# Weight chunks through two buffers of magnitudes and four raw ones, the loads in another order, and the first two steps reordered on every engine

## What is computed

```
_quant_weight(w):  s = max(|w|, row) / 127;  q = round(w / s)                    # wq, wo
_qlinear(..., W):  Wr = W[:, idx];  w_scale = max(|Wr|, row) / 448;  qw = fp8(Wr / w_scale)   # w_gate, w_up, w_down
q = w8a8(layernorm(x), wq, bq);  k = ctx @ wk.T + bk;  v = ctx @ wv.T + bv        # 16 heads of 32
o = softmax(q k^T / sqrt(32) + mask) v
x = x + tanh(g_xattn) * w8a8(o, wo, bo)
h = layernorm(x);  g, u = fp8linear(h, w_gate), fp8linear(h, w_up)                # 1408 wide
x = x + tanh(g_ffn) * fp8linear(silu(g) * u, w_down)
```

## Time and profile before

| | |
|---|---|
| runs before | 606.95 us median of 3 (601.56 to 607.03) |
| profiled execution | 608.15 us |
| its span | 606.4 us |
| busy share of the span | PE 87%, DVE 85%, ACT 79%, POOL 37% |
| granted TensorE clock, mean | 0.942 |
| step 0 / step 1 / a steady step | about 75.7 / 68.7 / 59.2 us |

### The profile page before, as it was taken

How to read it: one execution, slowest core, us unless ns; L and a number is a source line. 1 busy time by engine, 2 the same in 40 slices (tenths; PEclk the granted TensorE clock), 3 DMA queues, 4 the chain that set the end, 5 groups by cost and what they waited for, 6 DMA issues and landing times.

```text
span 606.4 us, 10842 instructions
## 1 busy us (share of the span) xinstructions
PE 525.3 (87%) x3456; PEld 332.3 (55%) x3456; DVE 513.5 (85%) x1290; ACT 477.2 (79%) x1160; POOL 223.4 (37%) x210
## 2 busy tenths in 40 slices
PE   0667878798999999999999999999999998877834
PEld 0655556556755675567556755765576555443311
DVE  3699985879889988998999899979997996599794
ACT  0697996999888898888988898889798987683341
POOL 1332333002281438234724471546164513361420
PEclk9898996998999999999999999999999998685888
DMA  7822523110001010101010101010100000000000
GB/s 273 273 88 70 157 70 97 69 53 2 36 1 54 36 36 2 52 36 36 2 53 36 35 2 54 36 36 1 53 37 1 1 2 35 1 2 0 35 1 35
DMA packets 15240, 28.75 MB, mean 47 GB/s; under 512 B 3792, under 2 KB 5840, under 8 KB 15184
## 3 DMA queue, kind: packets, MB, share of 16 engines
q1 hardware_dynamic: 8640, 14.68, 7.2%
q0 software_dynamic: 3488, 12.85, 6.5%
q10 hardware_dynamic: 3056, 0.54, 0.5%
HBM read 23.87 MB, written 4.19 MB: 46 GB/s over the span
## 4 chain that ended last, share of the span: by engine, by line
PE 51%; DVE 21%; ACT 13%; issue 10%; ACTq 2%; DMA 1%; POOL 1%; DVEq 0%; POOLq 0%
PE bank_s L794 7%; PE bank_t L853 7%; PE bank_u L814 5%; PE bank_g L814 5%; PE bank_a L801 4%; PE bank_g L801 4%; DVE prob L1265 3%; PE bank_o L895 2%; DVE q L1180 2%; DVE t_sb L1175 2%; DVE t_sb L1219 2%; ACT prob L597 2%; PE bank_a L825 2%; PE bank_g L1029 2%; DVE ts L1450 2%
## 5 line engine op out<-in xcount | busy, mean ns | idle before, releaser
L597 ACT ACTIVATE prob<-prob,neg_max 128x256 f32<-128x256 f32 x256 | 127.2, 503 | 2.8 <-DVE neg_max L1265 2.7
L1265 DVE CUSTOM_DVE_ANT_0 prob<-bank_s,mask_sb 128x256 f32<-128x256 f32 x256 | 96.6, 420 | 22.1 <-PE bank_s L794 8.5
L608 ACT ACTIVATE probT<-bank_t 128x512 f32<-128x512 f32 x128 | 73.5, 588 | 19.9 <-PE bank_t L853 16.7
L385 POOL TENSOR_TENSOR up<-up,wgu_scale 128x512 f32<-128x512 f32 (+1 forms) x42 | 54.7, 1303 | 89.5 <-ACT up L577 89.5
L853 PE MATMUL bank_t<-ident,prob 128*128 128x128 f32 x512 | 79.2, 283 | 8.8 <-ACT prob L597 7.9
L853 PEld LDWEIGHTS bank_t<-ident,prob 128*128 128x128 f32 x512 | 59.3, 143 | 35.9 <-issue 17.2
L794 PE MATMUL bank_s<-kf,qf 32*128 32x256 f32 x512 | 75.3, 413 | 3.0 <-DVE neg_max L1265 2.9
L794 PEld LDWEIGHTS bank_s<-kf,qf 32*128 32x128 f32 x512 | 45.2, 190 | 27.0 <-issue 18.3
L395 POOL TENSOR_TENSOR up<-gate,up 128x512 f32<-128x512 f32 (+1 forms) x42 | 54.4, 1295 | 4.6 <-DVE gate L1325 1.9
L400 POOL TENSOR_TENSOR x<-x,y 128x512 f32<-128x512 f32 x14 | 19.6, 1398 | 97.8 <-DVE y L1463 97.8
L597 ACT ACTIVATION_READ_ACCUMULATOR prob<-prob,neg_max 128x1 f32 x256 | 49.9, 195 | 0.0
(11 more groups left out here) (254 smaller groups left out, 1212.7 us busy)
## 6 DMA issues: line engine op xcount, KB each, us to landing
x_in<-in_x_dram SPq DMA_DIRECT2D x8, 512.0 KB, 3.4
c_in<-in_ctx_dram SPq DMA_DIRECT2D x8, 512.0 KB, 3.5
out_dram<-x POOLq DMA_DIRECT2D x7, 512.0 KB, 3.2
t_sb<-in_L_ffn_w_down_dram POOLq DMA_DIRECT2D x4, 704.0 KB, 6.0
mask_sb<-in_mask_BxSxS_ff_dram SPq DMA_DIRECT2D x8, 256.0 KB, 3.7
kf<-in_L_xattn_wq_dram SPq DMA_DIRECT2D x1, 1024.0 KB, 6.6
probT<-in_L_xattn_wk_dram SPq DMA_DIRECT2D x1, 1024.0 KB, 13.3
qf<-in_L_xattn_wv_dram SPq DMA_DIRECT2D x1, 1024.0 KB, 17.5
```

The costliest lines, as they stand in the source:

```text
L385: pool.tensor_tensor(up[:, c % 2, 0:w], up[:, c % 2, 0:w], wu_scale[:, off:off + w], ALU.mult).then_inc(f["u_scaled"], 1)
L597: ins = act.activation(prob[:, head_par, t, :], prob[:, head_par, t, :], ACT.Exp, bias=neg_max[:, head_par, t:t + 1], scale=-1.0, accum_ou ...
L608: act.activation(probT[:, (slot + 3) % 4, :, :].rearrange("p a b -> p (a b)"), T_BANK[(slot + 1) % 2][:, :], ACT.Copy).then_inc(s["turned_ ...
L1265: ins = dve.tensor_tensor_reduce(prob[:, hp, t, :], S_BANK[hp][:, t * L:(t + 1) * L], mask_sb[:, hb, t, :], -1.0, 3.4e38, ALU.add, ALU.min ...
```

## The change

The edits go together:

- **Units and buffers.** Magnitudes alternate between `mag` with `th` (even k) and `q8_last` seen as 32-bit (odd k). Raw data go through four buffers in turn, k % 4. The rounded unit goes to a new tile `unit_h`, alternating, no longer to `up`. The order of units is down 0, down 1, pair 0, pair 1, down 2, down 3, pairs 2 to 10.
- **Waits.** `mag_unit(k)` waits for unit k-2 to be rounded, the load of unit k for unit k-4, the second pass of `round_unit(k)` for unit k-2 to be turned.
- **Loads.** SP issues down 0 and down 1 ahead of wq, wk after wq, then x and ctx, wv, the gates, bo, bv, wo, bk, bq and the mask. ACT issues the index alone. POOL's first load is pair 0.
- **Order.** The prologue's parts become blocks of step 0, and steps 0 and 1 have another order on every engine. Steady steps and the tail are as before.

```diff
+        unit_h = sb("unit_h", [P, 2, I], BF16)
-        UNITS = [("down", 0), ("down", 1)] + [("pair", c) for c in range(IC)] + [("down", r) for r in range(2, CC)]
+        PAIRS = [("pair", c) for c in range(IC)]
+        UNITS = [("down", 0), ("down", 1)] + PAIRS[0:2] + [("down", 2), ("down", 3)] + PAIRS[2:]
+        raws = (t_sb[:, 0, :], t_sb[:, 1, :], gate[:, :, :].rearrange("p a b -> p (a b)"), x2[:, :, :].rearrange("p a b -> p (a b)"))
         def unit_raw(k):
+            return raws[k % 4][:, 0:2 * C if UNITS[k][0] == "pair" else I]
         def unit_parts(k):
+            w = 2 * C if UNITS[k][0] == "pair" else I
+            if k % 2:
+                return [(0, w, q8_last[:, :].bitcast(F32))]
...
         @block.sync
+            for k in range(2):
+                sp.dma_start(unit_raw(k), w_down[UNITS[k][1] * P:(UNITS[k][1] + 1) * P, :]).then_inc(unit_loaded(k)[0], 16)
             load8("q", wq)
-            load8("k", wk)
...
         @block.gpsimd
-            load_unit(0)
-            pool.wait_ge(s["x_loaded"], 16)
-            load_unit(1)
             pool.wait_ge(s["index_loaded"], 16)
             load_unit(2)
             load_unit(3)
-                        pool.wait_ge(s["wf_ready"], 1 if k == 4 else k - 2)
+                        pool.wait_ge(s["wf_ready"], k - 3)
...
             def mag_unit(k):
-                need(act, s["wf_ready"], k)
+                need(act, s["wf_ready"], k - 1)
             def round_unit(k):
-                need(dve, s["wf_turned"], k - 1 if UNITS[k][0] == UNITS[k - 1][0] == "pair" else k)
+                need(dve, s["wf_turned"], k - 1)
```

More of the change, by code:

```diff
@@ L252, in unit_loaded @@
         def unit_loaded(k):
-            kind, n = UNITS[k]
-            return (s[f"wf_loaded_{n % 3}"], 32 * (n // 3 + 1)) if kind == "pair" else (s[f"wf_loaded_{3 + n % 2}"], 16 * (n // 2 + 1))
+            if k < 2:
+                return s[f"first_loaded_{k}"], 16
+            return s[f"wf_loaded_{k % 4}"], sum(32 if UNITS[j][0] == "pair" else 16 for j in range(k % 4, k + 1, 4) if j >= 2)
         def unit_at(u, first):
@@ L311, in _, with load_unit @@
         def _(pool):
+            def load_unit(k):
+                kind, n = UNITS[k]
+                if kind == "down":
+                    pool.dma_start(unit_raw(k), w_down[n * P:(n + 1) * P, :]).then_inc(unit_loaded(k)[0], 16)
+                else:
+                    for m, src in enumerate((w_gate, w_up)):
+                        pool.indirect_dma_start(unit_raw(k)[:, m * C:(m + 1) * C], None, src,
+                                                bass.IndirectOffsetOnAxis(ap=index[:, n:n + 1], axis=0)).then_inc(unit_loaded(k)[0], 16)
             for name in ("out_ready",):
@@ L324, in _ @@
             pool.wait_ge(s["pow_const"], 1)
-            def load_unit(k):
-                kind, n = UNITS[k]
-                if kind == "down":
-                    pool.dma_start(unit_raw(k), w_down[n * P:(n + 1) * P, :]).then_inc(unit_loaded(k)[0], 16)
-                else:
-                    for m, src in enumerate((w_gate, w_up)):
-                        pool.indirect_dma_start(pair_raw[n % 3][:, m * C:(m + 1) * C], None, src,
-                                                bass.IndirectOffsetOnAxis(ap=index[:, n:n + 1], axis=0)).then_inc(unit_loaded(k)[0], 16)
-            load_unit(0)
-            pool.wait_ge(s["x_loaded"], 16)
-            load_unit(1)
             pool.wait_ge(s["index_loaded"], 16)
@@ L434, in _ @@
         def _(act):
+            act.dma_start(index[:, :], down_index.rearrange("(c p) -> p c", p=P), allow_slow_non_contiguous=True).then_inc(s["index_loaded"], 16)
             for name in ("tT_out_act", "u_ready"):
@@ L462, in mag_unit @@
                 act.wait_ge(s["wf_scaled"], 4 * k + 4)
-                need(act, s["wf_ready"], k)
+                need(act, s["wf_ready"], k - 1)
                 raw = unit_raw(k)
                 if UNITS[k][0] == "pair":
+                    m = unit_parts(k)[0][2]
                     for n in range(2):
-                        act.activation(mag[:, n, :], raw[:, n * C:(n + 1) * C], ACT.Abs, scale=wf_r[:, k % 3, 1, n:n + 1])
+                        act.activation(m[:, n * C:(n + 1) * C], raw[:, n * C:(n + 1) * C], ACT.Abs, scale=wf_r[:, k % 3, 1, n:n + 1])
                     for n in range(2):
@@ new lines, in first_step_order @@
+                k.pro_turn_k(0); k.ctxT_turn(0); k.ctxT_turn(1); k.pro_turn_q(0); k.k_project_even(2)
+                k.k_project_odd(2); k.k_project_even(3); k.k_project_odd(3); k.unit_turn(2); k.xT_turn(4)
+                k.pro_turn_v(1); k.unit_turn(4); k.wo_scale_turn(5); k.xT_turn(5); k.pro_turn_o(4); k.unit_turn(6)
+                k.sx_turn(6); k.q_project_0(6); k.q_project_1(7); k.unit_turn(8); k.first_score(11); k.unit_turn(10)
+                k.v_project_low(10); k.head_score(13); k.head_turn(13); k.head_turn(14); k.unit_turn(12)
@@ L1227, in x2_job, with unit_scale_0, pro_scale_q, pro_k @@
                     return JOBS * B2 + t, mag[:, t, :], rows[:, t, :], xq[:, t, :], C
+                def unit_scale_0(slot):
+                    scale_unit(0)
+                def pro_scale_q(slot):
+                    scale8("q", 0)
+                def pro_k(slot):
+                    pro_evac("k")
+                def pro_int_q(slot):
+                    int8("q", 0)
+                def unit_round_0(slot):
+                    round_unit(0)
+                def pro_q(slot):
+                    pro_evac("q")
                 def pro_v(slot):
                     pro_evac("v")
+                def pro_scale_o(slot):
                     scale8("o", 1)
```

179 lines of the change are left out of this document (88 added, 91 removed).

## The result

The changed kernel takes 602.8 us (median of 20 runs, 597.94 to 606.12), the kernel before beside it 608.32 us (20 runs, 601.27 to 611.27). The ratio is 0.9924, with a 95% interval of 0.9895 to 0.9953; a second series gave 0.9911 (0.9872 to 0.9949). So the change saves 0.8 to 0.9%, some 5 us, where I had forecast 8.4. The profiled execution takes 601.54 us with a span of 599.8.

What follows compares the result with a forecast made beforehand. Steps 0 and 1, with ACT's start and idle time, were taken as what the change can shorten: 7.4 start + 112.5 work + 12.9 + 3.2 idle = 136.0 against 144.4 us, 8.4 earlier, so 599 us; range 591 to 607.

Steps and rivals of the forecast that it cites:

- The new wait: Step 0, ACT at the tanh of the gates: idle from 22 to 31 us for bq, 9 us, bounds 5 and 14.
- ACT idle from there to step 1: Rest of step 0 behind the tanh: 1.8 us of idle time on ACT, bounds 0.5 and 4.
- Start of ACT: Step 0: ACT's first activation at 7.4 us instead of 16.7, 9.3 us earlier, bounds 6.4 and 9.
- only some 4 of it were the constants' fault: Tanh wait: PE's k projection would release the copy only at 27.2 us anyway, so 5 of 9 us aren't the constants'.
- I leave 1.2 us for what comes in its place, beside the other 2.0 us.: ACT in step 1: 3.2 us idle in place of 6.0, bounds 1.5 and 6.5.
- away whole: ACT's 4.0 us wait for step 1's k projection, traced to late unit 10, goes entirely with earlier loading.
- Steady steps and tail follow unchanged: Behind step 2's begin: everything keeps its length, so the 8.4 us gained ahead carries to the total.
- rivals of small gain at 605: Steps 0 and 1: constants' wait takes most of the gain (chance 0.22), or the change does little (0.08); both 605 us.
- late constants: Tanh in step 0, first rival at 605: bq lands at 36 us in place of 31, taking back 5 us.
- a new wait in step 1 worth 3.3 us: Step 1, first rival at 605: a new wait as long as the old one takes back 3.3 us.
- The deeper gain: Rival, steps 0 and 1: small constants before 27.2 us and 1.5 us idle in step 1 give 593 us; chance 0.15.
- no wait of 4 us on L528: Sign in step 1's profile: ACT's 4.0 us wait for the k projection no longer appears.

Runs made afterwards that it cites:

- const_sp: The changed kernel, with SP issuing the gates, bk and bq right behind wk instead of behind wv and wo; 598.31 us, ratio 0.981.
- the pair of repeats: The changed kernel and its version with constants right behind wk, each unedited and once more on one chip; 601.39 us (0.9911) and 602.08 us (0.9891).
- old_act: The changed kernel, with ACT issuing all seven small loads again ahead of its first work, SP none; 604.34 us, ratio 0.9916.
- old_mag: The changed kernel, with magnitudes of unit k waiting for unit k-1 again, as with one buffer; 609.7 us, ratio 1.0008.
- old_step1: The changed kernel, with step 1 in its old order on every engine, except one exchange on PE; 607.72 us, ratio 0.9969.
- old_load: The changed kernel, with the load of unit k waiting for unit k-3, as with three raw buffers; 623.85 us, ratio 1.025.
- before_again: The kernel before the change, unedited, run and profiled once more; 609.31 us, ratio 0.9987.
- its variants: Constants-early version with DVE scaling unit 2 ahead of wo (600.95 us), or POOL's step 1 bias addition moved later (603.05 us) or behind all loads (603.22 us).

## Why the prediction came out too high

What came out too high is the gain. The new wait at the tanh was foreseen rightly, and a size behind it was not. Set against the changed kernel's two executions, from the tanh on:

| us | forecast | first | second |
|---|---|---|---|
| ACT starts | 7.4 | 7.38 | 7.30 |
| tanh, bq landed | 31 | 31.16 | 32.06 |
| ACT idle from there to step 1 | 1.8 | 3.4 | 1.2 |
| ACT idle in step 1 | 3.2 | 5.4 | 5.0 |
| ACT's work from the tanh on | 100.0 | 99.7 | 99.6 |
| step 2 begins | 136.0 | 139.84 | 137.85 |

The idle times are the windows' lengths less ACT's busy time; for the second execution the window from 31.2 to 73.9 has 40.67 of 42.7 us busy, of which 0.86 idle lie ahead of the tanh.

- **Start of ACT**: right to 0.1 us, with the down unit at 5.28 and DVE's 2.1 us, but in part by luck. The DMA moved 304 and 323 GB/s from 2 to 4 and 4 to 6 us, not 250 and 209, so some 1.0 MB had moved when the 0.72 MB of down 0 were there: a higher rate, shared with the loads behind it.
- **The new wait**: its end at 31 was right; it is 10.7 us and not 9 because ACT came at 20.5 and not 22, which costs nothing. The rate of 0.37 MB a us held to 20.4 us (373 GB/s from 7.4 on); over the whole stretch to the tanh, 7.4 to 31.16, it was 344. That only some 4 of it were the constants' fault held as well: const_sp gives 3.2 us back at the rounding of x, and the pair of repeats 4.3 (33.26 and 28.95). By the 358 GB/s of the Trainium skill ("DMA: Bandwidth & Descriptors", Specifications) the prediction's estimate had bq at about 32. The two executions have 31.16 and 32.06, so the landing decides nothing. The window of 373 GB/s stands above the figure, which is no contradiction: the page works it out as half of a stack's 716 GB/s, one of two cores' shares, and this kernel runs on one core. The prediction took it for a limit of a core alone.
- **Where the gain came from**: here the reasoning was weaker than the sum. The sum booked 9.3 us to the start and took 3.7 back in idle time of step 0. old_act shows that a start 7.5 us later gives the same time. On ACT's account of the first execution the 4.6 us are 9.3 of start, less 6.2 of more idle time in step 0, plus 0.9 of less work, which the prediction had put at nothing, and 0.6 of less idle time in step 1. What the gain can't do without is the second magnitude buffer (old_mag, 6 to 8 us), the order of step 1 (old_step1, 5 to 7 at the begin of step 2, some 3 by the ratios) and the fourth raw buffer (old_load, 20). Added up, these prices are several times what the change brings: at least the buffers are worth this only in the new order. The order of step 0 and the early index were not undone by themselves.
- **The step that failed: "I leave 1.2 us for what comes in its place, beside the other 2.0 us."** Idle time of ACT in step 1 is 5.4 and 5.0 us in place of 3.2. The k copy's wait is 2.1 and 0.7, but the turned units (1.6 and 1.8), the masks (1.3 and 0.5) and, in the second execution, the turned probabilities (1.8) stand beside it. So beside the k copy's wait there are 3.3 and 4.3 us, where the prediction had "the other 2.0 us". That ACT, with a shorter step, meets PE and DVE sooner than they are ready is my reading and was not tested. This term is 2 of the 3.8 and 1.9 us by which the two executions begin step 2 later than forecast. The rest is 1.6 us more idle time in step 0 in the first, and in the second a tanh 1.1 us later, less 0.6 us of idle time.
- **The base of that step.** I had traced 4.0 us to one chain in one execution. before_again has no wait of ACT on the k copy in step 1 at all; its ACT idles there 69.2 - 65.2 = 4.0 us in place of 6.0, and more in step 0, with the same begin of step 2 (144.93). So that wait was real but not the kernel's constant price, and against this second execution the changed kernel's 5.4 and 5.0 us are not even a gain. The prediction let this one wait go "away whole" and carried the 2.8 us into its sum.
- **The rest of the line.** "Steady steps and tail follow unchanged" held for the steady steps (355.5 and 355.8 us). The tail varies by 4 us between executions, as much as half of the forecast gain.
- **Range and rivals.** 602.8 lies in the range of 591 to 607, and nearer to the rivals of small gain at 605 than to 599. Their first mechanism, late constants, did not occur (bq at 31, not 36); of their second, a new wait in step 1 worth 3.3 us, half to two thirds did (2.2 and 1.8). The deeper gain wanted early constants and 1.5 us of idle time in step 1. const_sp met the first alone, and 593 did not follow.
- **What the profile was to show.** PE turned the context of step 1 at 78.83 and 79.12, not 72, as the prediction overlooked what now stands ahead of that turn in PE's list; the index landed at 10.1 (9.4 us behind its issue at 0.73), not 13.5; no wait of DVE for a landing in step 1, a granted clock of 0.92 there, and no wait of 4 us on L528: as said. Step 1's length, from PE's first block on, was 64.4 and 62.0, below the mark of 66.

**What stays open.** Early constants: the three series of const_sp have 0.981, 0.9891 and 0.9913, the changed kernel's two 0.9924 and 0.9911. Weighted by their intervals that is 0.988 to 0.992, about 2 us, barely more than they can tell, and in the one series that had both on one chip their intervals overlap. It fits with step 1 beginning some 2 us earlier in two of three executions (PE's first group product at 76.00 and 75.77, in the third at 78.90, against 77.82 and 78.12 in the changed kernel), and const_sp and its variants are the fastest versions I have, but it is not shown beyond doubt. What DVE's stop with the releaser "remote" is, stays open too: it stood in 3 of the executions, ahead of the same instruction, and in none of the others of these kernels. In all three the k projection shortly ahead of it had taken 3.62 us and not 1.89, but so had it in const_sp, which has no such stop. The three begin step 2 at 139.84, 139.47 and 143.79, later than the executions of the same kernel without it, where there are such.

## What to carry to other kernels

A start moved forward is worth only what the next wait on that engine leaves of it: walk to that wait and to what it waits for before the time saved at the start is booked, and move the small constants with the start. Buffers and an order that uses them are one change: undone singly, one buffer took back all of the gain and the other four times as much, and the order of an engine's list decides how long a load may take. Before a wait of 2 us is given a cause, take a second profile of the same kernel: here the same instructions began step 2 at 135.2, 138.0 and 143.8.
